# A ViT tower on one NeuronCore: six blocks of the first feed-forward placed inside the end of the first attention, and the experts' weight rounding, splits and search steps placed elsewhere

## The reference

```python
h = _L0_tok_ref(x, ...)                      # patch embedding
h = h + _L0_attn_ref(_layernorm(h), ...)     # 16 heads of 64, causal
h = h + _L0_ffn_ref(_layernorm(h), ...)      # 256 -> 1024 -> 256, the "first feed-forward"
h = h + _L1_attn_ref(_layernorm(h), ...)     # 16 heads of 64
h = h + _L1_ffn_ref(_layernorm(h), ...)      # 8 experts, 256 -> 1024 -> 256
```

```python
h = jnp.einsum('bsd,df->bsf', x, w1) + b1
h = float2fix(h, 8)                          # round to 1/256
h = pwlin_gelu_basic(h, 8, 8)                # line between knots of exact GELU
out = jnp.einsum('bsf,fd->bsd', h, w2) + b2
return float2fix(out, 8)
```

```python
kth_val = jnp.sort(logits.reshape(-1))[expert_k - 1]
mask = (logits >= kth_val)
gates = logits * mask
```

## Time and profile before

| quantity | value |
|---|---|
| time, median of 3 runs | 980.0 us (979.19 to 980.0) |
| time of the profiled execution | 979.99 us |
| its span in the trace | 978.2 us |
| TensorE busy | 933.1 us (95%) |
| weight loads busy | 863.7 us (88%) |
| VectorE busy | 579.8 us (59%) |
| ScalarE busy | 542.0 us (55%) |
| GpSimd busy | 154.8 us (16%) |
| first attention, end of its last matmul | 237.7 us from the span's start |
| first feed-forward, TensorE's first and last matmul | 238.3 to 318.7 us |
| experts, TensorE's first matmul | 524.3 us |

### The profile page before, as it was taken

The page is one execution under the profiler, slowest core; times in us unless marked ns, Lnnn a source line. Parts: engine busy times, 40 slices in busy tenths (PEclk is TensorE's granted clock), DMA queues, the critical chain, the costliest instruction groups (busy, mean ns, idle before and its releaser), DMA issues.

```text
span 978.2 us, 18614 instructions
## 1 busy us (share of the span) xinstructions
PE 933.1 (95%) x7135; PEld 863.7 (88%) x7135; DVE 579.8 (59%) x1251; ACT 542.0 (55%) x1569; POOL 154.8 (16%) x173
## 2 busy tenths in 40 slices
PE   6999999999799999999999899999999999999998
PEld 6877888788677878888889898999999999999998
DVE  5566575746999574665656677555453545444342
ACT  4666464653764664655555526556664647555452
POOL 0332121210000122221210000431110111110111
PEclk9999999999999999999999999999999999999999
DMA  8310000002000210000002011111011111100001
GB/s 325 130 44 2 1 1 1 2 1 87 1 1 1 87 44 1 2 2 1 2 7 81 15 73 44 44 43 46 2 44 44 44 44 44 44 1 1 1 14 38
DMA packets 8796, 34.46 MB, mean 35 GB/s; under 512 B 642, under 2 KB 5122, under 8 KB 5380
## 3 DMA queue, kind: packets, MB, share of 16 engines
q1 hardware_dynamic: 8708, 33.28, 9.4%
HBM read 32.06 MB, written 1.22 MB: 34 GB/s over the span
## 4 chain that ended last, share of the span: by engine, by line
issue 32%; PE 24%; POOL 5%; DVE 5%; ACT 2%; POOLq 0%; DVEq 0%; ACTq 0%
PE D L574 8%; PE O L574 7%; POOL h L362 4%; PE O L740 2%; PE T L726 2%; PE S L715 1%; PE S L574 1%; DVE hid L1528 1%; ACT hid L1100 1%; DVE wslot L1128 1%; PE S L709 1%; POOL h L374 1%; ACT work L1096 1%; PE O L854 1%; POOL vbuf L372 1%
## 5 line engine op out<-in xcount | busy, mean ns | idle before, releaser
L1528 DVE TENSOR_TENSOR hid<-work,hid 128x300 fp32r<-128x300 f32 (+1 forms) x256 | 139.1, 565 | 191.9 <-ACT hid L1100 191.6
L574 PE MATMUL O<-hid,wslot 128*128 128x300 f32 (+3 forms) x1680 | 240.6, 301 | 0.0
L574 PEld LDWEIGHTS O<-hid,wslot 128*128 128x128 f32 x1680 | 233.0, 189 | 0.6
L574 PE MATMUL D<-xn,wslot 128*128 128x300 f32 (+3 forms) x1368 | 222.4, 307 | 1.4 <-ACT hid L1100 1.4
L574 PEld LDWEIGHTS D<-xn,wslot 128*128 128x128 f32 x1368 | 197.7, 189 | 6.1 <-ACT hid L1100 2.7
L1096 ACT ACTIVATE work<-D,prm 128x300 f32<-128x300 f32 (+1 forms) x128 | 66.7, 521 | 179.7 <-PE D L574 179.7
L996 ACT ACTIVATE probs<-S,negmax 111x111 f32<-111x111 f32 (+1 forms) x352 | 117.5, 358 | 53.5 <-DVE negmax L1293 53.2
L553 POOL TENSOR_TENSOR probs<-probs,rsum 111x444 f32<-111x444 f32 (+1 forms) x88 | 80.9, 920 | 379.8 <-DVE rsum L1301 379.8
L574 PE MATMUL S<-xn,wslot 128*128 128x300 f32 (+3 forms) x864 | 136.2, 305 | 0.0
L574 PEld LDWEIGHTS S<-xn,wslot 128*128 128x128 f32 x864 | 125.3, 191 | 0.3
L362 POOL TENSOR_TENSOR h<-h,work 128x300 f32<-128x300 f32 (+1 forms) x56 | 49.5, 905 | 287.6 <-DVE work L1547 287.6
(11 more groups left out here) (174 smaller groups left out, 1165.0 us busy)
## 6 DMA issues: line engine op xcount, KB each, us to landing
raw<-in_moe SPq DMA_DIRECT2D x16, 1024.0 KB, 4.8
raw<-in_attn SPq DMA_DIRECT2D x7, 1024.0 KB, 4.9
work<-in_x SPq DMA_DIRECT2D x2, 1008.0 KB, 8.0
w2f<-in_attn SPq DMA_DIRECT2D x1, 1024.0 KB, 12.6
raw<-in_ffn SPq DMA_DIRECT2D x1, 1024.0 KB, 4.8
w2f<-in_ffn SPq DMA_DIRECT2D x1, 1024.0 KB, 4.9
raw<-in_x SPq DMA_DIRECT2D x2, 504.0 KB, 5.2
out<-h SPq DMA_DIRECT2D x3, 300.0 KB, 2.8
```

Source lines behind the costliest of these rows:

```text
L574: mm = pe.matmul(psum, a, b, start=(first and k == 0), stop=(k == 3 * n - 1))
L1528: nc.vector.tensor_tensor(moe_hid(s, 1), moe_g(s)[:, 0:w], moe_hid(s, 0).bitcast(F32), ALU.subtract).then_inc(m_hid, 1)
```

## The change

It moves work; apart from two more loads of ScalarE's function tables nothing of weight is added, and only matmuls that nobody reads (15 of `keep_busy`) are removed.

1. TensorE issues blocks 0 to 5 of the feed-forward in steps 22 and 23 of the first attention, in place of `keep_busy` there. Banks are used in the order S0, S1, D0, D1, and `project_out(3, 1)` goes to T0, so that it frees the others.
2. ScalarE loads GELU's table and moves blocks 0 and 1 in step 22, ahead of `high_out(21)`. VectorE issues `ff_find(0)` and `ff_part(0)` there, and the last `add_out`s only inside the pairs 1 and 2.
3. `ff_round` moves between the next pair's `ff_slope` and the next but one's `ff_find`.
4. The halves of `ff_down` stand apart, and one chunk earlier: `(c-1, 0)` after the sixth block of chunk c, `(c-2, 1)` after its second.
5. Chunk 3's layer norm is spread over pairs 3 to 9, with two table loads around `inv_root(1, 3)` between the GELUs of pairs 7 and 8.
6. The splits of the next weights move (w1's to steps 20 and 21, the next one's to step 22 and pair 1).
7. Experts: `high_part` stands at the first block of a chunk, before the wait for that block; the splits of expert 1's weights stand at n = 1 to 4 beside the seventh and eighth search step of each n; each `search` stands before `moe_low` and not behind it; the first `sum_counts` stands two blocks earlier.

```diff
@@ TensorE, attention, steps 22 and 23
                     if u == NUNIT:
-                        keep_busy(*ahead, 6)
+                        if l == 0:
+                            ff_up1(0)
+                        else:
+                            keep_busy(*ahead, 6)
                     if 0 <= u - 1 < NUNIT:
                         transposes(2 * u - 1)
                     if u == NUNIT + 1:
-                        keep_busy(*ahead, 5)
+                        if l == 0:
+                            ff_up1(2)
+                            ff_up1(3)
+                        else:
+                            keep_busy(*ahead, 5)
+                    elif u == NUNIT and l == 0:
+                        ff_up1(1)
...
+                    if l == 0 and u == NUNIT + 1:
+                        ff_up1(4)
+                        ff_up1(5)
                     if due is not None:
                         project_out(due, 1)
@@ TensorE, the feed-forward
-            for c in range(NC):
-                ff_up(c)
-            ff_down(NC - 2)
-            ff_down(NC - 1)
+            for s in range(6, NC * KH):
+                c, m = s // KH, s % KH
+                ff_up1(s)
+                if (c, m) == (0, KH - 1):
+                    mean(1, 3)
+                if (c, m) == (1, 4):
+                    variance(1, 3)
+                if c >= 1 and m == 5:
+                    ff_down(c - 1, 0)
+                if c >= 2 and m == 1:
+                    ff_down(c - 2, 1)
+                if (c, m) == (NC - 1, 3):
+                    mean(2, 0)
+            variance(2, 0)
+            ff_down(NC - 2, 1)
+            for dc in range(KD):
+                ff_down(NC - 1, dc)
@@ ScalarE, attention and feed-forward
+                    if l == 0 and u == NUNIT:
+                        nc.scalar.preload_act_table_set("gelu_and_others")
+                        ff_load(0)
+                        ff_load(1)
                     if u >= 1:
                         high_out(u - 1)
...
-                if p == -1:
+                if p == 3:
                     square(1, 3)
+                if p == 7:
+                    nc.scalar.preload_act_table_set("natural_log_exp_and_others")
                     inv_root(1, 3)
+                    nc.scalar.preload_act_table_set("gelu_and_others")
@@ VectorE, the feed-forward
+            for p in range(1, NP + 2):
+                if p <= NP:
                     ff_slope(p - 1)
+                if p >= 2:
+                    ff_round(p - 2)
                 if p < NP:
                     ff_find(p)
...
-                    ff_round(p - 1)
-                if p == 0:
+                if p == 1:
+                    low_quarter(FIRST_W + 6, 2)
+                    low_quarter(FIRST_W + 6, 3)
+                if p in (1, 2):
+                    add_out(NC - 1, p - 1)
+                if p == 3:
                     center(1, 3)
+                if p == 9:
                     finish(1, 3)
-                if KH <= p < NP and p % (KH // 2) == 0:
-                    ff_out(2 * p // KH - 2)
+                if p in (7, 11, 15):
+                    ff_out1(p // 4 - 1, 0)
+                if p in (10, 14):
+                    ff_out1(p // 4 - 2, 1)
...
-            finish(2, 0)
-            ff_out(NC - 2)
+            root = newton(2, 0)
+            ff_out1(NC - 2, 1)
+            apply(2, 0, root)
             for k in range(SPLITS):
                 low_quarter(FIRST_W + 7, k)
-            ff_out(NC - 1)
+            for dc in range(KD):
+                ff_out1(NC - 1, dc)
             attention(1)
@@ ScalarE, the experts
+                if s in (2 * KH, 3 * KH):
+                    high_part(FIRST_W + W_MOE + s // KH)
+                if e >= 1 and e + 1 < E and c in (1, 2) and m == 0:
+                    high_part(FIRST_W + W_MOE + 2 * e + 1 + c)
                 act.wait_ge(m1_mm, s + 1)
-                if s in (10, 12):
-                    high_part(FIRST_W + W_MOE + s // 2 - 3)
-                if e >= 1 and e + 1 < E and (c, m) in ((0, 1), (1, 4)):
-                    high_part(FIRST_W + W_MOE + 2 * e + 2 + c)
@@ VectorE, the experts
-                if n in (2, 3) and m < SPLITS:
-                    low_quarter(FIRST_W + W_MOE + n, m)
...
+                if m % 2 == 0 and 1 <= n <= 4 and s > KH:
+                    search(8 * (n - 1) + m // 2)
                 moe_low(s)
...
-                if m % 2 == 0 and 1 <= n <= 4 and s > KH:
-                    search(8 * (n - 1) + m // 2)
                 if m == KH - 1 and 1 <= n <= 4:
                     for i in range(4, 8):
                         search(8 * (n - 1) + i)
                         if i % 2:
                             moe_out1(*steps[n - 1], (i - 4) // 2)
+                        if i >= 6:
+                            low_quarter(FIRST_W + W_MOE + 2 + (n - 1) // 2, 2 * ((n - 1) % 2) + i - 6)
```

More of the change, by code:

```diff
@@ L146, in vit_tower @@
         BH = BD + BS
+        BF = BS + BD
         BJ = BD + [BO[1]]
@@ L341, in ff_bufs @@
             if p % 3 == 0:
-                flat = vbuf[:, :, :].rearrange("p s n -> p (s n)")
-                three = [pair(flat, k) for k in range(3)]
+                three = [ffs[:, 2 * k:2 * k + 2, :] for k in range(3)]
             elif p % 3 == 1:
@@ L347, in ff_bufs @@
             else:
-                three = [ffs[:, 2 * k:2 * k + 2, :] for k in range(3)]
+                flat = vbuf[:, :, :].rearrange("p s n -> p (s n)")
+                three = [pair(flat, k) for k in range(3)]
             return [t[:, :, 0:w] for t in three]
@@ L844, in ff_down @@
-            def ff_down(c):
-                a, w = CHUNKS[c]
-                pe.wait_ge(ff_hid, KH * (c + 1))
-                if c == 0:
-                    pe.wait_ge(w2_in, 16)
-                for dc in range(KD):
-                    if c >= 1:
-                        pe.wait_ge(ff2_ev, KD * (c - 1) + dc + 1)
-                    w2 = w2f[:, :].rearrange("p (a n) -> p a n", n=D)
-                    for i in range(KH):
-                        mm = pe.matmul(BO[dc][:, 0:w], w2[:, i, dc * P:(dc + 1) * P],
-                                       work[:, KH * (c % 2) + i, 0:w], start=(i == 0), stop=(i == KH - 1))
-                    mm.then_inc(ff2_mm, 1)
@@ L899, in moe_up @@
                         i = 8 * (n - 1) + m // 2 - 1
+                        if n == 1 and m <= 3:
+                            i = 0 if m == 1 else -1
                         if 0 <= i < 32:
@@ L1037, in _ @@
             high_part(FIRST_W + 2)
-            attention(0)
             def ff_load(s):
@@ L1056, in ff_knots @@
                 nc.scalar.activation(y1, y1, ACT.Gelu, bias=c_knot1[:, 0:1], scale=1.0 / UNIT).then_inc(ff_y1, 1)
-            for p in range(-1, NP):
-                if p >= 0:
-                    ff_knots(p)
+            attention(0)
+            for p in range(NP):
+                ff_knots(p)
                 if p + 1 < NP:
@@ L1353, in attention @@
                         invert_sums(2 * u + 1)
+                    if l == 0 and u == NUNIT + 1:
+                        break
                     if due is not None:
@@ L1363, in attention @@
                         low_out(u - 1)
+                    if l == 0 and u == NUNIT:
+                        ff_find(0)
+                        ff_part(0)
                     if l == 1 and u == NUNIT + 1:
@@ L1380, in attention @@
                             low_quarter(tail_weight(l)[k // SPLITS], k % SPLITS)
-            attention(0)
+                return add_out
             def ff_find(p):
```

111 lines of the change are left out of this document (64 added, 47 removed).

## The result

The changed kernel takes 957.38 us (median of 4 runs, 956.99 to 958.55); the kernel before took 980.0 (979.19 to 981.09) beside it. The ratio is 0.9771, 95% interval 0.9754 to 0.9787. The forecast was 961.5, with a range of 957.0 to 968.5. The measured time lies 0.4 us above the lower end of that range and outside the forecast's own 959 to 964.5.

The account below looks back on a forecast made before the run. TensorE's list was taken as the time, so the change is worth the waits it removes less those it adds: 979.99 - 10.3 (first feed-forward) - 8.2 (experts) = 961.5 us, range 957 to 968.5.

Parts of the forecast that it names:

- End of the first attention: TensorE, after six feed-forward blocks issued there, is done at 240.0, or 240.2 with start-up gaps; 5.2 us ahead.
- The pair at 3.57 us: First feed-forward: moving ff_round away from ff_sum cuts VectorE's cost of a pair from 3.76 to 3.57 us.
- the loop is the bound: Feed-forward: ScalarE's loop exceeds 3.57 us and VectorE idles in each pair; +4, 965.5 us; chance 0.14.
- The first new wait: Feed-forward, at mean(1, 3) after block 7: TensorE waits 2.3 us for VectorE's add_outs.
- the one before `ff_down`: Feed-forward, after block 13: TensorE waits 1.3 us for VectorE's round(3) before the first ff_down.
- my walk: VectorE's feed-forward list followed instruction by instruction with prices from the trace, giving the term of -10.3 us.
- The stand behind the table loads: Between pairs 7 and 8 VectorE stands 1.3 us while ScalarE switches tables; hidden from TensorE.
- The term of the feed-forward: First feed-forward: TensorE reaches its end 11.8 us earlier, 1.5 given back at the second attention's third block; -10.3.
- slower by the clock: From the wait at mean(1, 3), TensorE stays at the lower clock for up to 62 us; 988 us; chance 0.03.
- I take out all five waits (5.4): Experts' first part, with the bisection: TensorE's five waits for counts go, 5.4 us of the -8.2 term.
- the five short waits ..., 1.4: Experts: waits of 0.3 us for ScalarE, from high_part at an expert's second block, go; 1.4 us.
- The rival at 957.5: Feed-forward bound by TensorE: VectorE's prices overlap better, giving -13 to -15 instead of -10.3; 957.5 us; chance 0.12.

Follow-up runs that it names:

- e_round: The changed kernel with ff_round put back directly behind ff_sum of its own pair: 958.78 us.
- again: The changed kernel itself, unaltered, timed once more beside the last three experiments: 957.79 us.
- e_ff: The changed kernel with the experts' part (part 7) undone, so parts 1 to 6 alone: 970.19 us.
- e_tables: The changed kernel with one more pair of table loads between pairs 7 and 8 on ScalarE: 960.70 us.

## Why the prediction was right, and where it was off

- **The number** is right by the width of the range. 957.4 lies outside the forecast's own 959 to 964.5; it is inside 957.0 to 968.5 because the lower end was put there for a rival whose mechanism did not occur.
- **What bounds the kernel** was right: TensorE's list, with its waits in the two stretches named. The change emptied the experts' waits and left the five forecast in the feed-forward.
- **End of the first attention** (six blocks by 240.2). Less the start's 1.2 us, block 6 starts at 240.0, so this was right.
- **The pair at 3.57 us**: right, by the trace and by `e_round` (3.77 without the move). Rival "the loop is the bound" falls. What the move is worth in the end was not shown to be the 3 us of 16 pairs; the runs say 1.0 to 1.9.
- **The first new wait** was 1.81, forecast 2.3; the one before `ff_down` 0.82 for 1.3. VectorE's second `add_out` came 0.6 us earlier than my walk had it.
- **The stand behind the table loads**: 1.19, forecast 1.3. It was not quite right that ScalarE only interrupts VectorE there: ScalarE's own chain is the bound for some 7.8 us.
- **The term of the feed-forward**: -11.0, forecast -10.3. The kind is right; the walk was 0.7 too slow, of which 0.25 is the last wait. It assumed no slow stretch, and the profiled execution had none; `again`, which had one, stands at -10.5.
- **Clock**: no rule by the length of a wait alone holds. The rival "slower by the clock" had the right place, and a slow stretch did come in 4 of the 8 profiled executions with that wait, but it costs 0.5 us. The rule of the Trainium skill that the prediction quoted beside it (TensorE: Matmul & The Clock Gate, What's actually happening: the throttled state is the default), as quoted there, gives no forecast here: the same wait of 1.81 us went both ways.
- **The experts: the step that failed** is "I take out all five waits (5.4)" and "the five short waits ..., 1.4", that is, pricing a wait at its listed idle time. The term was mis-sized: -12.15 in place of -8.2. Five short waits listed at 1.4 gave 2.63. Five waits for counts with their slow stretch, 6.8, gave 9.5, because each costs about 0.25 more than listed, and three of the five have a second late count behind them, 0.34 us each, that the list doesn't name. The slow stretch itself was priced about right for a change that takes out the next wait as well: the two rows behind the first wait took 5.35 us (542.10 to 547.45) for twice 1.89, 1.6 more, forecast 1.4. Where the next wait stays, as in `e_ff`, it is worth 0.75.
- **Causes in the experts**: the two roundings at n = 1 were rightly named for the first wait. The prediction did not see that the later roundings also made the waits at n = 4 (2.9 us), nor how the rest divides.
- **The rival at 957.5** met the number by chance. Its mechanism, 13 to 15 us from the feed-forward, did not occur.

## What to carry to other kernels

Price a wait of a pipelined engine by the distance between the starts of the same instructions with and without it, not by the idle time that is listed: here 0.28 us listed were 0.54, and 0.5 us were 1.7. Behind a late step of a serial loop look for a second one that is late by less than the overlap. A gap in one engine can be filled only if the other engine's chain that makes it is not itself the bound; moving work within the span of that chain changes nothing.

## What the runs showed of the hardware that I had not expected

A stretch at the lower clock is a matter of the execution as well as of the program: with the same wait of 1.81 us at the same place, 4 of 8 profiled executions had one, and one and the same program went both ways. No wait that was listed under 1.8 us in the first feed-forward was followed by one, nor was one of 1.94 in `e_tables` or of 2.88 in `e_clock`. A comparison of two profiles should therefore leave such a stretch out of what the edit did. And the start of the program varies by 1.5 us between executions (8.7 to 10.2 us to the first matmul), which is as much as several of the edits here are worth.
